# Graph layer on one core: the product e1 of the edge stage as four products of 64 rows by 64 columns

## The reference

```
h  = silu(edge_attr_16 @ Wfc1/4);  w = h @ Wfc2/8     -> w0 (64) w1 (64) w2 (32) w3 (32)
f0 = x0 @ Wl1_0 ...;  f1 = x1 @ Wl1_1 ...  (64 scalars, 32 vectors of a node)
e0 = f0[src];  e1 = f1[src];  sh0, sh1 = edge_attr_4[:, :1], [:, 1:4]
mid0 = w0*e0*sh0      mid1 = w3 * (e1 . sh1)/sqrt(3)
mid2 = w1*e0*sh1      mid3 = w2*e1*sh0
n0..n3 = mean of mid0..mid3 over the edges of each node
out = sc + (scal @ Wa) * [scal @ Wl2_s, vec @ Wl2_v];  x = layernorm(x + out)
```

## Time and profile before

| | |
|---|---|
| median of 3 runs | 1088.9 us |
| profiled execution | 1078.5 us, of which the span is 1076.7 us |
| busy: PE / DVE / ACT / POOL | 948.9 / 852.3 / 643.5 / 743.3 us |
| edge stage, node stage | about 680 us, about 395 us |
| mean granted TensorE clock | 0.976 |

### The profile page before, as it was taken

The page is one execution under the profiler, slowest core; times in us unless marked ns, Lnnn a source line. Parts: engine busy times, 40 slices in busy tenths (PEclk is TensorE's granted clock), DMA queues, the critical chain, the costliest instruction groups (busy, mean ns, idle before and its releaser), DMA issues.

```text
span 1076.7 us, 26917 instructions
## 1 busy us (share of the span) xinstructions
PE 948.9 (88%) x7944; PEld 806.5 (75%) x7944; DVE 852.3 (79%) x2596; ACT 643.5 (60%) x2055; POOL 743.3 (69%) x809
## 2 busy tenths in 40 slices
PE   3588888887988888988888889899999999999995
PEld 2477777775777777777777778788888888888884
DVE  3476777785777777777777778699999999999997
ACT  1243444443444444444444445389999999999998
POOL 6556455555555555555555551399999999999994
PEclk9799899999999999999999999899999999999998
DMA  5244443333344444433334332589999999999983
GB/s 163 65 137 134 128 119 106 102 108 92 105 116 97 125 129 132 129 102 108 109 111 115 108 105 77 155 260 288 299 294 304 287 295 295 302 291 304 288 287 152
DMA packets 87515, 186.32 MB, mean 173 GB/s; under 512 B 17646, under 2 KB 48138, under 8 KB 87371
## 3 DMA queue, kind: packets, MB, share of 16 engines
q1 hardware_dynamic: 48411, 87.64, 26.6%
q10 hardware_dynamic: 20016, 61.15, 16.9%
q0 software_dynamic: 18944, 35.81, 13.6%
HBM read 119.58 MB, written 64.95 MB: 171 GB/s over the span
## 4 chain that ended last, share of the span: by engine, by line
PE 69%; ACT 13%; issue 12%; DVE 2%; another core or an unknown queue 1%; DMA 1%; ACTq 1%; POOL 0%; SPq 0%; POOLq 0%; DVEq 0%
PE ps L762 12%; PE ps L668 11%; PE ps L686 8%; PE ps L706 7%; PE ps L772 6%; PE ps L673 6%; PE ps L655 5%; PE ps L704 5%; ACT t_sb L799 4%; ACT fin L845 4%; PE ps L751 3%; PE ps L653 3%; ACT z L807 2%; PE ps L647 2%
## 5 line engine op out<-in xcount | busy, mean ns | idle before, releaser
L567 POOL DMA_INDIRECT gat<-turned,srcs x196 | 185.4, 946 | 205.5 <-PE ps L655 153.9
L567 POOL DMA_INDIRECT gat<-spread,srcs x196 | 185.7, 947 | 63.3 <-issue 63.0
L822 ACT ACTIVATE e_sb<-ps 128x512 f32<-128x512 f32 x196 | 106.4, 594 | 185.8 <-PE ps L673 107.0
L963 DVE TENSOR_TENSOR z<-ps,sha 128x96 f32<-128x96 f32 x392 | 98.7, 252 | 121.7 <-ACT z L807 107.9
L762 PE MATMUL ps<-win,hot 60*128 60x162 f32 x2352 | 190.8, 307 | 4.7 <-ACT agg L871 1.8
L668 PE MATMUL ps<-t_sb,wt 128*128 128x256 f32 x392 | 122.1, 426 | 78.0 <-ACT t_sb L799 56.9
L762 PEld LDWEIGHTS ps<-win,hot 60*128 60x128 f32 x2352 | 168.5, 188 | 23.2 <-DVE hot L1276 19.0
L706 PE MATMUL ps<-wy,mid 128*128 128x161 f32 x784 | 185.3, 318 | 0.0
L845 ACT ACTIVATE fin<-res,shift,rstd 128x160 f32<-128x160 f32 x386 | 169.5, 510 | 13.3 <-DVE shift L1284 9.0
L797 ACT ACTIVATE h_sb<-ps 128x128 f32<-128x128 f32 x196 | 57.2, 292 | 180.0 <-PE ps L655 170.0
L969 DVE SCALAR_TENSOR_TENSOR msg<-ps,sha,z 128x161 f32<-128x161 f32 x392 | 151.0, 385 | 13.9
(11 more groups left out here) (100 smaller groups left out, 1662.8 us busy)
## 6 DMA issues: line engine op xcount, KB each, us to landing
win<-rows SPq DMA_DIRECT2D x392, 114.6 KB, 3.7
rows<-msg SPq DMA_DIRECT2D x98, 326.0 KB
out<-fin ACTq DMA_DIRECT2D x47, 640.0 KB, 5.9
xin<-x_g ACTq DMA_DIRECT2D x92, 322.0 KB
gat<-turned,srcs POOLq DMA_INDIRECT x196
gat<-spread,srcs POOLq DMA_INDIRECT x196
eas<-ea_t SPq DMA_DIRECT2D x7, 384.0 KB, 3.6
xin<-x_g SPq DMA_DIRECT2D x6, 322.0 KB
```

The costliest lines, as they stand in the source:

```text
L567: pool.indirect_dma_start(out=gat[:, slot, first:first + of.shape[1]], out_offset=None, in_=of, in_offset=bass.IndirectOffsetOnAxis(ap=src ...
```

## The change

e1 becomes four products of 64 rows by 64 columns of weights, one on each quarter of the array. The second tile's halves are swapped: rows 0 to 63 give columns 64 to 127 and the other way round, so no two of the four share a quarter. `e_ps` of tile 1 has its halves swapped from there on, so Wfc2 (pack_weights) and the weights of `combine` for tile 1 (new columns W_Y1B) are swapped too. The waits ahead of e1 now all stand ahead of the first of the four.

```
+W_Y1B = W_SB + P
+WC = W_Y1B + VEC + 1 + MUL0
...
                     if q >= 1:
                         pe.wait_ge(e_out[t], q)
-                    nc.tensor.matmul(e_ps[:, t, 2 * P:4 * P], wt[:, W_E1:W_E1 + P],
-                                     t_sb[:, b, 1 + t].rearrange("p k e -> p (k e)"),
-                                     start=True, stop=True)
+                for n in range(2):
+                    for t in range(2):
+
+                        half = slice(n * HALF, (n + 1) * HALF)
+                        made = slice((n + t) % 2 * HALF, ((n + t) % 2 + 1) * HALF)
+                        nc.tensor.matmul(e_ps[made, t, 2 * P:4 * P],
+                                         wt[half, W_E1 + half.start:W_E1 + half.stop],
+                                         t_sb[half, b, 1 + t].rearrange("p k e -> p (k e)"),
+                                         start=True, stop=True)
...
-                        pe.wait_ge(wy_ready, 8)
+                        pe.wait_ge(wy_ready, 12)
...
+                    of = (W_Y1, W_Y1B)[t] - W_YA
                     nc.tensor.matmul(y[:, t, W_Y1 - W_YA:YW], mid[:, q % 2, t, 1, k, :],
-                                     wy[:, W_Y1 - W_YA:W_SA - W_YA],
+                                     wy[:, of:of + VEC + 1 + MUL0],
...
-            nc.vector.tensor_scalar(wy[0:MUL1, W_Y1 - W_YA:W_SA - W_YA], wt[0:MUL1, W_Y1:W_SA],
-                                    inv_fc * inv32 * inv96 * 3 ** -0.5, None,
-                                    ALU.mult).then_inc(wy_ready, 1)
-            for m in range(3):
-                part = slice((m + 1) * MUL1, (m + 2) * MUL1)
...
+            for t, of, width in ((0, W_Y1, W_SA - W_Y1), (1, W_Y1B, WC - W_Y1B)):
+                for m in range(4):
+
+                    part = slice((m + 2 * t) % 4 * MUL1, ((m + 2 * t) % 4 + 1) * MUL1)
+                    nc.vector.tensor_scalar(wy[part, of - W_YA:of - W_YA + width],
+                                            wt[part, of:of + width],
```

More of the change, by code:

```diff
@@ L87 @@
 W_SB = W_SA + P
-WC = W_SB + P
+W_Y1B = W_SB + P
+WC = W_Y1B + VEC + 1 + MUL0
 LAST = D - P
@@ L775, in step @@
                                             xt[:, b1, GROUP, :],
-                                            wy[:, W_SB - W_YA:WC - W_YA], start=True, stop=True)
+                                            wy[:, W_SB - W_YA:W_Y1B - W_YA], start=True, stop=True)
                     last.then_inc(sc_ready, 1)
@@ L1126, in _ @@
                                     None, ALU.mult).then_inc(wy_ready, 1)
-            nc.vector.tensor_scalar(wy[0:MUL1, W_Y1 - W_YA:W_SA - W_YA], wt[0:MUL1, W_Y1:W_SA],
-                                    inv_fc * inv32 * inv96 * 3 ** -0.5, None,
-                                    ALU.mult).then_inc(wy_ready, 1)
-            for m in range(3):
-                part = slice((m + 1) * MUL1, (m + 2) * MUL1)
-                nc.vector.tensor_scalar(wy[part, W_Y1 - W_YA:W_SA - W_YA], wt[part, W_Y1:W_SA],
-                                        inv_fc * inv32 * inv96, None,
-                                        ALU.mult).then_inc(wy_ready, 1)
+            for t, of, width in ((0, W_Y1, W_SA - W_Y1), (1, W_Y1B, WC - W_Y1B)):
[3 more added lines that the diff above has]
+                                            wt[part, of:of + width],
+                                            inv_fc * inv32 * inv96 * (1 if m else 3 ** -0.5),
+                                            None, ALU.mult).then_inc(wy_ready, 1)
             nc.vector.tensor_scalar(wy[0:MUL0, W_SA - W_YA:W_SB - W_YA], wt[0:MUL0, W_SA:W_SB],
@@ L1138, in _ @@
                                     inv32, None, ALU.mult).then_inc(wy_ready, 1)
-            nc.vector.tensor_scalar(wy[:, W_SB - W_YA:WC - W_YA], wt[:, W_SB:WC], inv32,
+            nc.vector.tensor_scalar(wy[:, W_SB - W_YA:W_Y1B - W_YA], wt[:, W_SB:W_Y1B], inv32,
                                     None, ALU.mult).then_inc(wy_ready, 1)
@@ L1306, in pack_weights @@
         col = W_W + P
-        w[rows, col:col + MUL1] = Wfc2[:, P + MUL1:]
-        for m in range(3):
-            w[rows, col + (m + 1) * MUL1:col + (m + 2) * MUL1] = Wfc2[:, P:P + MUL1]
+        for m in range(4):
+            made = col + (m + 2 * s) % 4 * MUL1
+            part = Wfc2[:, P:P + MUL1] if m else Wfc2[:, P + MUL1:]
+            w[rows, made:made + MUL1] = part
         for c in range(2):
@@ L1321, in pack_weights @@
     w[0:MUL1, W_Y1 + VEC + 1:W_SA] = Wl2_s[MUL0:]
+    for half in range(2):
+        other = slice((1 - half) * HALF, (2 - half) * HALF)
+        w[half * HALF:(half + 1) * HALF, W_Y1B:WC] = w[other, W_Y1:W_SA]
     w[0:MUL0, W_SA:W_SA + MUL0] = Wsc0
```

## The result

The changed kernel takes 1102.67 us, the median of 4 runs (1099.93 to 1103.5), against 1089.77 for the kernel before (the three runs behind the 1088.9 and a fourth). The ratio is 1.0127, with a 95% interval of 1.0091 to 1.0163. The change makes this kernel slower by 1.3%. I had forecast 1088 with a range to 1099, so the time lies outside, on the slow side.

What follows compares the result with a forecast made beforehand. The prediction took POOL's gather bursts, not PE, to bound the edge stage. Its terms, 0 - 2 - 1 + 2 + 0 = -1 us, taken off the median, gave 1088, with a range of 1079 to 1099.

Steps and rivals of the forecast that it cites:

- The loop: Edge stage: `t_ready` reaches waiters about 1.05 us after POOL's gather burst, so POOL, not PE, sets the 6.46 us period.
- 80 quads that wait for msg: ... Gain 0.: e1 in 80 of 98 quads: the four products start where the second started, 0.63 us before and after, gain 0.
- hidden by the 1.4 above: e1: products running two at a time (+0.43) or one by one (+1.29) would not show within PE's 1.4 us slack.
- What was taken for slack: PE in an edge-stage quad: about 1.1 us to spare, and its turn could end up to about 1.4 us later unseen.
- The four side by side: e1: all four quarter products run at once in 0.43 us, each having its own quarter of the array.
- The size of PE's gain: e1 in the 18 other quads, where PE can run through: 0.23 us less each, period 5.15, taken as -2 us.
- Instructions: PE's instruction stream: four more MATMUL and LDWEIGHTS each per quad, 9.5% more, 3 more packets, taken as +2 us.
- Half clock and start: Four or five quads at 1.2 GHz gain more at e1, -1 us; DVE's four extra wy products at the start, 0.
- No difference: Whole kernel: the forecast itself, with stalls as they are, a change below 0.3% (3.3 us); chance 0.49.
- PE decides after all: Edge stage: the release follows PE's own end, so e1's saving shows, -22 us (1066) or -6; chance 0.24, at about 1083.
- More stalls: PE's unexplained idle places: more of them, or one shifting against the gathers, +4 to +12 us, 1093 to 1101; chance 0.21.
- the rival that the four don't run side by side: e1: products two at a time or one by one, with no slack on PE, +42 to +126 us, 1131 to 1215; chance 0.06.

Runs made afterwards that it cites:

- old_waits_first: The kernel before, its two e1 products unchanged, with all waits ahead of the first: 1088.69 us, ratio 1.0104 on a chip where updates are held.
- changed_third: The changed kernel as it is, run again on the third chip, where updates are held: 1090.88 us, ratio 1.0086 to the kernel before.
- quarters_twice: The changed kernel with e1's four products issued twice over, on a chip where nothing is held: 976.59 us, ratio 1.0223 to the kernel before.
- by_tile: The changed kernel with the four products tile by tile, each pair behind its own tile's waits: 1089.18 us, ratio 1.0114 to the kernel before.
- msg_last: The changed kernel with the wait for tile 1's msg moved last in the code ahead of e1: 1087.34 us, ratio 1.0115 to the kernel before.
- quarters_twice_2: The changed kernel with e1's four products issued twice over, repeated on another chip, which held nothing: 976.91 us, ratio 1.0227 to the kernel before.

## Why the prediction was wrong

**The loop.** That the edge stage follows POOL's bursts and not PE was right on holding chips: 0.44 us a quad more or less on PE (old_waits_first, changed_third) leaves the on-time period at 6.54, while one wait on POOL changes the period to 6.29, and no gathers at all to 5.22. It was not right as a rule for this kernel: on free chips PE sets the period. And PE's timing does count where it decides in which of two ways the loop runs.

**The step that failed: "80 quads that wait for msg: ... Gain 0."** It counted what is late at e1 and let all behind it be "hidden by the 1.4 above", on the reading that only `t_ready` reaches its waiters late. The runs showed that e0's update can be held too: where e0 ends 0.18 us after the start of the third gather it passes in 0.05 us, where it ends 1.15 after it, it takes 2.2. Whether it is held decides between two steady ways of running, 6.50 and 6.7 to 6.8 us a quad. The kernel before never settled in the slower one in its trace; the changed one has 75 held quads in its own, 54 on the third chip.

**What was taken for slack.** PE's 1.1 to 1.4 us was not free: from 307.86, where e0 ended, to the start of the fourth gather at 308.94 are 1.08 us, and an e0 that ends near the end of them is held. I had priced a later PE, but not an earlier one or one in another place.

**The four side by side: right.** The first records of e1's four products start between 314.93 and 314.95, quarters_twice gives 0.43 for four, and from e1's weights to those of e0 it is 315.52 - 314.89 = 0.63, the figure that I gave. The Trainium skill ("TensorEngine Tiling (Array Packing)", Key Properties) says that different tiles can load weights and multiply in parallel, and this case agrees, with 0.43 for four. The Trainium skill (the same page, Gotcha 1: PSUM Pressure) says that different row tiles cannot access the same PSUM bank at the same time. Rows 0 to 63 and 64 to 127 do write to the same banks here, and no run shows a cost of it, with each on its own half of the partitions: four products one bank at a time would have taken 0.86 or more, and they take 0.43. The measurement decides, and the rival that the four don't run side by side is out. (Three quarters of an old product met zeros, not half as I wrote of W_E1; the half of the array that the change leaves out is all zeros.)

**The size of PE's gain: mis-sized.** I gave 0.23 where PE runs through, a period of 5.15. It is 0.16, 5.22. With the old products behind all waits the period is 5.66, so the four products give 0.44 and the moved waits take 0.28. With the order or the places of the waits put right the gain is 0.275 (by_tile, msg_last). The working had no term for that order: `msg` ends at 314.29 + 0.39 = 314.68 and e1's weights start 0.21 later, where the earlier trace rows have 0.04. The row of msg:

```profile
314.29 0.39 DVE L977 SCALAR_TENSOR_TENSOR msg<-ps,sha,z 128x161 f32<-128x161 f32 x1
```

**Instructions.** The queue has 69 packets in the whole trace against 66 before, the 3 more that I gave. That they cost 2 us is neither shown nor excluded.

**Half clock and start.** The mean granted clock is 0.975 after and 0.976 before, and wy's four products cost nothing that the traces show, as said.

**The rivals.** *No difference* was my forecast and is out. *PE decides after all* was wrong on holding chips and right on free ones, where the ratio is 0.991 to 0.994 and not the 0.980 that 22 us would be: part is given back in longer waits. *More stalls* named the sign and nearly the size (1093 to 1101) but not the place: it put them at PE's long idle places, and they are in the steady quads. That the size is near is luck.

**What stays open.** Why the changed kernel falls into the held way so often and the kernel before doesn't. It is not the place of the waits (msg_last 56, by_tile 45 held) nor their cost. Both ways are steady in one and the same kernel, and the long disturbances, near q = 10, 23, 33, 62 and 86 in all these traces, are what switches between them. So a trace has only about six stretches to count, not 98 quads: in before all six are on time, in the changed kernel one of six in either trace, in msg_last two. Nor is there one fixed place in the burst from which updates are held: in changed_third e0 ends 0.35 after the third gather's start in 28 quads in a row and is on time, and in four others with the same 0.35 (q = 26, 28, 89 and 91), near a disturbance, e_sb is 2.8 to 2.9 us late. Across the runs on holding chips, held quads against PE's period behind the last gather are 8 at 5.38, 21 at 5.66, 54 and 75 at 5.22, 45 and 56 at 5.105: all kernels with four products have many, both with two have fewer. Whether a kernel with four products and a slow PE would have few is what quarters_twice_2 was to tell. Since each number comes from one trace of few stretches, chance has a large part that I can't size. The ratios of these kernels, 1.0086 to 1.0127, are the same within their intervals, whatever the count. And the untraced executions of before may well have more held quads than 8. Why a gather holds updates, and why only on some chips, no row shows.

## What to carry to other kernels

Before an edit on the busiest engine, ask whether the same stretch runs faster with the other engine's stream taken out: a kernel without its gathers, one run, would have shown here that some 140 of 1081 us belong to them, and at what period PE alone runs. Look at when an update leaves one engine and when its waiter starts; where the two lie over 1 us apart, count that for every update, since a stage can have two steady periods, and an edit that costs nothing in one of them may go with a move to the other. And measure on more than one chip: the same edit is 0.9% slower on one and 0.8% faster on the next.

## What was not expected of the hardware

- On some chips TensorE's updates that fell late in a burst of four indirect DMAs of GpSimd (0.95 us each, 1.25 apart) reached their waiters about 2.2 us late, about 1.1 us after the last DMA. Those that fell 0.18 us into the third DMA passed in 0.05 us, as they do without the gathers.
- This differs between chips, all else being the same: the kernel before takes 1076 to 1090 us on some, 954 to 955 on others, at a granted clock of 0.976 and 0.993 in its two traces. Without the gathers the changed kernel takes 941 on both.
- Among several waits ahead of one product their order matters: weights start 0.22 us after the last event in one order and 0.05 to 0.12 in another, 0.12 us a quad.
- Products of 64 rows by 64 columns in fp32 on the four quarters of the array take 0.43 us for all four at 256 columns each, although two of them write to each PSUM bank at once, each to its own half of the partitions.
